# First expert's weights loaded during attention's output steps, into exchanged places of SBUF

## The chip, the cores and the metric

The kernel runs on all 8 cores of one Trainium2 chip. Each core takes one of the 8 sequences (2048 tokens of 1024 numbers) and works alone; the cores exchange nothing. The time is device microseconds of the slowest core, so a change counts only as far as it shortens the core that ends last.

## The reference

One layer: an attention block and a mixture-of-experts block, each with a layer norm before it, one after it, and a residual.

```python
x = x + layernorm(attn(layernorm(x), w_lhs, w_rhs))
x = x + layernorm(ffn(layernorm(x), ...))

def attn(x, w_lhs, w_rhs):            # one head, no projections
    scores = einsum('nsd,ntd->nst', x * w_lhs, x * w_rhs)
    return einsum('nst,ntd->nsd', softmax(scores, axis=2), x)

def ffn(xf):
    shared = silu(xf @ w1.T) * (xf @ w2.T) @ w3.T       # hidden 4096
    s = sigmoid(xf @ router_w.T)                        # 8 experts
    gates = s * one_hot(top_k(s + bias, 2)).sum(-2)     # 2 per token
    routed = sum_e((silu(h1_e) * h2_e * gate_e) @ w3_e.T)   # hidden 1024
    return shared + routed
```

## The kernel before, in words

A core's tokens are 16 tiles of 128. The program has these stages:

1. **Norm and scores** (0 to about 185 us): layer norm, transposes, attention's scores and their exponentials. The exponentials lie in four blocks `P_T[0..3]`, one for each 4 tiles; the normed tokens in `n1_tm[0..15]`.
2. **Attention's output steps** (185 to about 310 us), one for each tile `g`. `av(g)` is 48 matmuls of `P_T[g // 4]` with all of `n1_tm`. `y1` and `y2` on VectorE form the second residual stream `x2t` and its moments, with two small powers on GpSimd between them (`rsqrt`, L392); SyncE stores `x2t` to DRAM (`x2s`) and loads the input tile of step `g + 4`. `n2a` and `n2t` norm and transpose it for the FFN. From `g = 6` on, 4 tiles at a time are routed, and from `g = 8` on GpSimd writes the normed rows to their experts' places in DRAM with two indirect DMAs a tile (`scatter(g - 8)`, L694). `n2a(g)` writes a row buffer of 10, and waits until the scatter of tile `g - 10` has landed.
3. **Units and experts** (310 to about 1440 us). The shared FFN is cut into 10 units `u` of 3 or 5 hidden tiles (11 pieces of weights, `load_s_piece`). After each of the units 0 to 7 stands one expert. `p1` makes a hidden tile for 512 tokens (matmuls into `h1`, `h2`; Silu on ScalarE `sg`; the product on VectorE `SG`), `p2` multiplies by `w3` into a bank `ob`, and VectorE copies or adds the bank to the accumulator `acc[0..15]` (L828, L830). An expert runs one turn ahead of a loop and then as many turns as its rows have further blocks of 128.
4. **End**: gathers of the experts' results into `acc`, the last norm, the output.

**Where the order comes from.** Every engine's instructions are written in program order, with waits on semaphores. GpSimd has one DMA queue (queue 0, also called software dynamic): the weights are f32 in DRAM and are cast to bf16 by the DMA, and the scatters go through the same queue, behind one another. SyncE has its own (queue 1, hardware dynamic). In unit 0 the routing of the last tiles is still under way: the list `hooks` puts a piece of it behind each `p1`, among them the scatters 8 to 15, then `zeros` (8 indirect DMAs that clear the rest of each expert's last block), then `blocks_begin`: SyncE waits until every scatter and `zeros` have landed, reads 17 numbers, and loads the first expert's first block `xst` (L1077). PE needs that block at `e_X` (transposes `xps<-xst`, L889), one `p1` before the end of unit 0.

**The first expert's weights.** An expert's weights are two halves `e_all[0]`, `e_all[1]` of 12 KB a partition, 24 KB in bf16, each loaded by three DMAs of 1 MB (counted in bf16). Before the change `e_all[0]` lies at 68 to 92 KB of a partition, over `n1_tm`, which PE reads until `av(15)` has ended. So its load for expert 0 stands behind step 15 on GpSimd, ahead of the scatters 8 to 15. The second half lies at 92 to 116 KB and is loaded by `s1_load`, behind `zeros`, with the next shared piece after it. The accumulators lie at 116 to 180 KB, over `P_T[1..3]` and free input buffers.

Of the kernel before, what the change touches and what calls it, by code (L numbers as in the profile page):

```python
# [5 lines left out]
F32 = mybir.dt.float32  # L6
# [7 lines left out]
P = 128  # L14
D = 1024
# [5 lines left out]
KB = 1024  # L21
NT = 16
# [28 lines left out]
def build_program():  # L51
# [11 lines left out]
    we_d = nc.dram_tensor("we", [2 * NEXP, P, 12 * KB], F32, kind="ExternalInput").ap()  # L63
# [11 lines left out]
    def sb_at(name, shape, dtype, off):  # L75
        fb = int(np.prod(shape[1:])) * mybir.dt.size(dtype)
        assert 0 <= off and off + fb <= ARENA_B, (name, off)
        return nc.alloc_sbuf_tensor_at(name, shape, dtype, offset=SB_BASE + off)
# [19 lines left out]
    NB2 = len(n2tm)  # L98


    s_off = [32 * KB, 50 * KB, 104 * KB]
    e_off = [68 * KB, 92 * KB]

    s_all = {(sl, n): sb_at(f"sall_{sl}_{n}", [P, n * 3, KB], BF16, s_off[sl])
             for unit in UNITS for p, sl in unit for n in [S_PIECES[p]]}
# [2 lines left out]
    e_all = [sb_at(f"eall_{h}", [P, 12, KB], BF16, e_off[h]) for h in range(2)]  # L108
    e_w12 = [e_all[h][:, 0:8, :].rearrange("p (k c2) (c1 q) -> p k (c2 c1) q", k=2, q=512) for h in range(2)]
    e_w3 = [e_all[h][:, 8:12, :] for h in range(2)]  # L110
    acc = [sb_at(f"acc{i}", [P, D], F32, (116 + 4 * i) * KB) for i in range(NT)]
    ffn_off = [180 * KB]

    def sb_ffn(name, shape, dtype):
# [20 lines left out]


    NX2 = 5
    x2r = [sb_at(f"x2r{b}", [P, D], F32, (68 + 4 * b) * KB) for b in range(NX2)]
    osb = [sb_at(f"osb{b}", [P, D], F32, (88 + 4 * b) * KB) for b in range(4)]

    pp = SG_off
    def sb_seq(name, shape, dtype):
# [94 lines left out]
    def mksem(name):  # L237
        g = nc.semaphore(name)
        h = g.__enter__()
        sem_guards.append(g)  # L240
        return h
# [11 lines left out]
    S = {n: mksem(n) for n in names}  # L253
# [3 lines left out]
    def inc(s, n=1):  # L257
        cnt[_sem_name[id(s)]] += n
        return cnt[_sem_name[id(s)]]

    def cur(s):
        return cnt[_sem_name[id(s)]]
# [9 lines left out]
    def dma(eng, out_ap, in_ap, s):  # L272
        v = inc(s, 16)
        E(eng, lambda e, o=out_ap, i=in_ap, ss=s: e.dma_start(out=o, in_=i).then_inc(ss, 16))  # L274
        return v
# [11 lines left out]
    def load_table(idx):  # L287
        E("scalar", lambda e, idx=idx: e.add_instruction(
            mybir.InstLoadActFuncSet(name=nc.get_next_instruction_name(),
                                     act_func_set_id=idx, ins=[], outs=[])))  # L290
# [5 lines left out]
    def wt(eng, tok):  # L296


        if tok is None:
            return  # L300
        if tok[0] == "dec":
            E(eng, lambda e: e.wait_ge(S[tok[1]], tok[2]).then_inc(S[tok[1]], -tok[2]))  # L302
        elif tok[0] == "peek":
            W(eng, S[tok[1]], tok[2])
        elif waited.get((eng, tok[0]), 0) < tok[1]:
            waited[(eng, tok[0])] = tok[1]
            W(eng, S[tok[0]], tok[1])
# [22 lines left out]
    def load_s_piece(p):  # L330
# [4 lines left out]
            ws_d[p][:, n * 2 * KB:n * 3 * KB].rearrange("p (a b) -> p a b", b=KB), S[f"ws{sl}"])  # L335
        s_loaded[p] = (f"ws{sl}", cur(S[f"ws{sl}"]))

    def load_e_half(k, h):
        for q in range(3):
            dma("gpsimd", e_all[h][:, 4 * q:4 * q + 4, :],  # L340
                we_d[2 * k + h, :, 4 * q * KB:(4 * q + 4) * KB].rearrange("p (a b) -> p a b", b=KB),
                S[f"we{h}"])
        e_loaded[(k, h)] = (f"we{h}", cur(S[f"we{h}"]))

    s_loaded, e_loaded = {}, {}
    slot_of = {p: sl for unit in UNITS for p, sl in unit}
# [151 lines left out]
    for s in range(NT + 3):  # L498
# [10 lines left out]
        i = s - 3  # L509
# [18 lines left out]
    for g in ready:  # L528
# [6 lines left out]
    av_tok, den_tok, y_free, ry_tok, r2_tok, x2_tok, n2a_tok, tp2_tok, n2_tok, logit_tok = (  # L535
        {}, {}, {}, {}, {}, {}, {}, {}, {}, {})
# [150 lines left out]
    def scatter(i):  # L687
        b = i % NB2
        wt("gpsimd", idx_tok[i // NR])
        wt("gpsimd", n2a_tok[i])  # L690
        wt("gpsimd", z_done)
        for k in range(2):
            v = inc(S[f"sct{b}"], 16)
            E("gpsimd", lambda e, k=k: e.indirect_dma_start(  # L694
                out=xs_d[:, :], out_offset=bass.IndirectOffsetOnAxis(ap=idx[k][:, i:i + 1], axis=0),
                in_=n2tm[b][:].bitcast(I32), in_offset=None).then_inc(S[f"sct{b}"], 16))
        sct[i] = buf_free[b] = (f"sct{b}", v)
# [9 lines left out]
    for g in range(NT):  # L707
        av(g)
        y1(g)
        if g >= 1:  # L710
            n2a(g - 1)
        if g >= 6 and (g - 6) % NR == 0:
            for i in range(g - 6, g - 6 + NR):
                logits(i)
        if g >= 2:
            n2t(g - 2)
        y2(g)
        q, s = divmod(g - 6, NR)
        if q >= 0 and s == 0:
            route_a(q)  # L720
        if q >= 0 and s == 1:
            ranks(q)
        if q >= 0 and s == 2:
            route_b(q)
        if g >= 8:
            scatter(g - 8)
    load_table(TBL_SILU)

    def n2_turn(g):
# [4 lines left out]
        if g == NT - 1:  # L734
            for i in range(NT - NR, NT):
                logits(i)

    wt("gpsimd", av_tok[NT - 1])
    load_e_half(0, 0)


    BT, BX = 2, 3
# [58 lines left out]
    def p2(u, tb, b, ready):  # L801

        tiles = tiles_of[u]
        wt("tensor", ready)
        for tt in range(4):
            ti = tb * 4 + tt
            for h in range(2):
                k = banks[bank_i[0] % len(banks)]
                bank_i[0] += 1
                wt("tensor", bank_free[k])  # L810
                for j, (piece, sl, jl) in enumerate(tiles):
                    w = s_w3[sl, S_PIECES[piece]]
                    f = mm(ob[k][:], SG[b][j][:, tt * P:(tt + 1) * P], w[:, jl, h * 512:(h + 1) * 512],
                           j == 0, j == len(tiles) - 1)
                    if j == len(tiles) - 1:
                        t = put("tensor", f, "pe")
                    else:
                        E("tensor", f)
                wt("vector", t)
                a = acc[ti][:, h * 512:(h + 1) * 512]  # L820
                if u == 0 and ti == NT - 1:
                    wt("vector", x2_tok[NT - 2])
                if u == NEXP:
                    wt("vector", ya_tok[ti])
                if u == NEXP + 1:
                    wt("vector", yk_tok[ti])
                if u == 0:
                    bank_free[k] = put("vector", lambda e, a=a, k=k: e.tensor_copy(a, ob[k][:]), "dve")  # L828
                else:
                    bank_free[k] = put("vector", lambda e, a=a, k=k: e.tensor_add(a, a, ob[k][:]), "dve")  # L830
                add_tok[(u, ti)] = bank_free[k]
            if u == NSU - 1 and tb < 3:
                hooks.append(lambda ti=ti: final_stats(ti))
            elif u == NSU - 1:
                final_stats(ti)
        SG_free[b] = t
        return t
# [270 lines left out]
        state["zeros"] = ("s_zr", v)  # L1108

    def s1_load():  # L1110
        load_e_half(0, 1)
        for b in buf_free:
            wt("gpsimd", buf_free[b])
        load_s_piece(1)
# [90 lines left out]
    for u in range(NSU):  # L1205
        nt = len(tiles_of[u])
        for tb in range(4):
            b = nblk[0] % 2
            for j in range(nt):
                k = u - 1 if j == 0 and tb == 0 and 1 <= u <= NEXP else None  # L1210
# [12 lines left out]
                elif state.get("next_e") is not None:  # L1223
                    k = state.pop("next_e")
# [134 lines left out]
```

## Time and profile before

| What | Value |
|---|---|
| Time, median of 3 runs | 1485.11 us (1481.72 to 1492.14) |
| The profiled execution's own time | 1484.35 us |
| Its slowest core (core 5), span | 1482.8 us |
| The other cores' spans | 1455.5 to 1474.4 us |
| PE busy on core 5 | 1386.6 us, 94% |
| PE's granted clock, mean of core 5 | 0.983 |

The profile's page is of core 5. PE, the matrix engine, is the busy one. What one stage costs is read from its own stretch of the timeline; "idle before" in brackets is the time an engine stood still ahead of a row, and the name behind it what released it. The row of slices cuts the span in 40 slices of 37 us.

### The profile page before, as it was taken

To read this page: it belongs to the slowest core of one execution; us is meant where nothing else is said; L and a number is where in the kernel's file an instruction comes from. 1 tells how busy PE (TensorE), PEld (TensorE's weight loads), DVE (VectorE), ACT (ScalarE), POOL (GpSimd) and SP (SyncE) were. 2 spreads that over 40 slices of the span, in tenths; PEclk is the share of its full clock that TensorE was granted. 3 is DMA by queue.
4 is the path that set the end of the run, shared out by engine and by line. 5 is a ranking of instruction groups with operands and counts; after the bars stand their busy time and mean duration, and the time that the engine had idled before them with its cause. 6 is when DMAs were issued, how large, how long until landed. Compare 5 with 4: busy or idle time off the path is not lost. (4 is left out here: it accounts for less than half of the span.)

```text
span 1482.8 us, 21476 instructions; the slowest of 8 cores (1455.5 to 1482.8 us)
## 1 busy us (share of the span) xinstructions
PE 1386.6 (94%) x7324; PEld 644.1 (43%) x7324; DVE 606.0 (41%) x1208; ACT 288.5 (19%) x423; POOL 235.7 (16%) x245
## 2 busy tenths in 40 slices
PE   3999999996999999999999999999999997999993
PEld 2443345542444444444444444444444443444431
DVE  5520067864422223532243444344235341243557
ACT  4642311120012211012111111111211101211123
POOL 5510011354000001000101010000010222033236
PEclk9999999998999999999999999999999998999997
DMA  7910073559712216611484749191186899486235
GB/s 203 284 44 1 0 178 125 180 138 253 129 50 77 72 64 155 116 50 64 119 172 93 164 78 178 46 199 40 68 166 105 164 204 217 126 165 114 86 114 185
DMA packets 46224, 184.82 MB, mean 125 GB/s; under 512 B 6208, under 2 KB 6208, under 8 KB 38592
## 3 DMA queue, kind: packets, MB, share of 16 engines
q0 software_dynamic: 18464, 103.05, 35.9%
q1 hardware_dynamic: 27680, 80.72, 16.2%
q8 instruction: 49, 0.80, 0.2%
q14 instruction: 31, 0.25, 0.1%
HBM read 203.61 MB, written 55.75 MB: 175 GB/s over the span
## 5 line engine op out<-in xcount | busy, mean ns | idle before, releaser
L323 PE MATMUL ob<-sall,SG 128*128 128x512 bf16 x1024 | 235.0, 386 | 16.0 <-DVE acc L830 7.2
L830 DVE TENSOR_TENSOR acc<-acc,ob 128x512 f32<-128x512 f32 x288 | 187.0, 686 | 9.6 <-PE ob L323 8.2
L323 PEld LDWEIGHTS ob<-sall,SG 128*128 128x128 bf16 x1024 | 101.1, 99 | 143.1 <-issue 27.7
L274 POOL DMA_DIRECT2D eall<-we x48 | 25.7, 557 | 770.6 <-PE h1pb L323 769.5
L323 PE MATMUL ob<-eall,GT 128*128 128x512 bf16 x592 | 136.0, 384 | 0.0
L323 PE MATMUL h1pb<-n2fm,sall 128*128 128x512 bf16 x512 | 122.8, 383 | 9.3 <-DVE SG L790 9.3
L790 DVE TENSOR_TENSOR SG<-sg,h2pb 128x512 bf16<-128x512 f32 x64 | 44.0, 687 | 211.4 <-PE h2pb L323 183.4
L323 PE MATMUL stp<-n1fm,afm 128*128 128x512 bf16 x512 | 123.3, 384 | 0.0
L323 PE MATMUL h1pa<-n2fm,sall 128*128 128x512 bf16 x512 | 122.4, 382 | 0.6 <-DVE SG L790 0.6
L323 PE MATMUL h2pb<-n2fm,sall 128*128 128x512 bf16 x512 | 121.4, 380 | 0.0
L323 PE MATMUL h2pa<-n2fm,sall 128*128 128x512 bf16 x512 | 121.2, 380 | 0.0
L323 PE MATMUL avp<-n1tm,pt 128*128 128x512 bf16 x512 | 118.8, 377 | 0.0
L790 DVE TENSOR_TENSOR SG<-sg,h2pa 128x512 bf16<-128x512 f32 x64 | 44.0, 688 | 152.6 <-PE h2pa L323 144.1
L781 ACT ACTIVATE sg<-h1pb 128x512 f32<-128x512 f32 x64 | 38.1, 595 | 273.0 <-PE h1pb L323 257.3
L323 PEld LDWEIGHTS ob<-eall,GT 128*128 128x128 bf16 x592 | 57.4, 99 | 64.6 <-issue 2.9
L929 DVE COPY GT<-tps 128x1024 bf16<-128x1024 bf16 x37 | 25.6, 692 | 142.7 <-DVEq L302 142.7
L781 ACT ACTIVATE sg<-h1pa 128x512 f32<-128x512 f32 x64 | 38.1, 596 | 226.6 <-PE h1pa L323 211.6
L323 PEld LDWEIGHTS h1pb<-n2fm,sall 128*128 128x128 bf16 x512 | 50.3, 99 | 70.9 <-issue 12.2
L323 PE MATMUL h1pa<-eall,xT 128*128 128x512 bf16 x296 | 69.9, 379 | 11.5 <-PEq L302 11.5
L323 PEld LDWEIGHTS h2pb<-n2fm,sall 128*128 128x128 bf16 x512 | 50.3, 98 | 61.0 <-issue 1.1
L323 PEld LDWEIGHTS h1pa<-n2fm,sall 128*128 128x128 bf16 x512 | 49.9, 98 | 60.6 <-issue 2.4
L323 PEld LDWEIGHTS h2pa<-n2fm,sall 128*128 128x128 bf16 x512 | 49.9, 98 | 59.0 <-issue 0.8
(129 smaller groups left out, 1402.1 us busy)
## 6 DMA issues: line engine op xcount, KB each, us to landing
eall<-we POOLq DMA_DIRECT2D x48, 1024.0 KB, 27.2
ys<-ysb SPq DMA_DIRECT2D x37, 512.0 KB, 2.7
xr<-x SPq DMA_DIRECT2D x32, 512.0 KB, 8.1
sall<-ws POOLq DMA_DIRECT2D x10, 1536.0 KB, 39.1
xst<-xs SPq DMA_DIRECT2D x39, 260.0 KB, 2.8
ys<-zrow SPq DMA_DIRECT2D x16, 512.0 KB, 9.1
x2s<-x2t SPq DMA_DIRECT2D x16, 512.0 KB
x2r<-x2s SPq DMA_DIRECT2D x16, 512.0 KB, 4.2
```

Of the source, the lines that this page charges most:

```text
L274: E(eng, lambda e, o=out_ap, i=in_ap, ss=s: e.dma_start(out=o, in_=i).then_inc(ss, 16))
L323: return lambda e: e.matmul(out, lhsT, rhs, start=start, stop=stop, skip_group_check=True)
L781: ta = put("scalar", lambda e: e.activation(sg[pr][:], hp[pr][0][:], ACT.Silu), "act")
L790: tv = put("vector", lambda e: e.tensor_mul(SG[b][j][:], sg[pr][:], hp[pr][1][:]), "dve")
L830: bank_free[k] = put("vector", lambda e, a=a, k=k: e.tensor_add(a, a, ob[k][:]), "dve")
L929: give("vector", lambda e: e.tensor_copy(GT[:], tps[:]), "cr_gt")
```

## The change

- The accumulators `acc[0..7]` move to 68 to 100 KB, the place of `n1_tm`; `acc[8..15]` stay. The expert's halves move to 100 to 124 KB (over `P_T[0]` and half of `P_T[1]`) and 124 to 148 KB (the rest of `P_T[1]`, and `P_T[2]`). The third place for shared pieces and the buffers of the last stage (`x2r`, `osb`) move with them.
- The first half of expert 0 is loaded in three single DMAs of 1 MB behind the scatters of the steps 9, 10 and 11, once `av(7)` has ended; the second half likewise in the steps 13, 14 and 15, once `av(11)` has ended.
- The old loads behind step 15 and in `s1_load` are gone. VectorE's first copy into `acc` names a wait for `av(15)`; VectorE has waited for it already in step 15, and no instruction is added.

```diff
-    s_off = [32 * KB, 50 * KB, 104 * KB]
-    e_off = [68 * KB, 92 * KB]
+    s_off = [32 * KB, 50 * KB, 136 * KB]
+    e_off = [100 * KB, 124 * KB]
...
-    acc = [sb_at(f"acc{i}", [P, D], F32, (116 + 4 * i) * KB) for i in range(NT)]
+    acc = [sb_at(f"acc{i}", [P, D], F32, ((68 if i < 8 else 116) + 4 * i) * KB) for i in range(NT)]
...
-    x2r = [sb_at(f"x2r{b}", [P, D], F32, (68 + 4 * b) * KB) for b in range(NX2)]
-    osb = [sb_at(f"osb{b}", [P, D], F32, (88 + 4 * b) * KB) for b in range(4)]
+    x2r = [sb_at(f"x2r{b}", [P, D], F32, (100 + 4 * b) * KB) for b in range(NX2)]
+    osb = [sb_at(f"osb{b}", [P, D], F32, (120 + 4 * b) * KB) for b in range(4)]
...
+    def load_e_part(k, h, q):
+        dma("gpsimd", e_all[h][:, 4 * q:4 * q + 4, :],
+            we_d[2 * k + h, :, 4 * q * KB:(4 * q + 4) * KB].rearrange("p (a b) -> p a b", b=KB),
+            S[f"we{h}"])
+        e_loaded[(k, h)] = (f"we{h}", cur(S[f"we{h}"]))
+
     def load_e_half(k, h):
         for q in range(3):
...
+            load_e_part(k, h, q)
...
         if g >= 8:
             scatter(g - 8)
+
+        if 9 <= g <= 11:
+            wt("gpsimd", av_tok[7])
+            load_e_part(0, 0, g - 9)
+        if g >= 13:
+            wt("gpsimd", av_tok[11])
+            load_e_part(0, 1, g - 13)
...
-    wt("gpsimd", av_tok[NT - 1])
-    load_e_half(0, 0)
...
+                if u == 0 and ti == 0:
+                    wt("vector", av_tok[NT - 1])
...
     def s1_load():
-        load_e_half(0, 1)
         for b in buf_free:
```

**GpSimd in the steps 9 to 11.** `ry` and `r` are the two small powers of a step, `xs<-n2tm` its scatters, `eall<-we` a weight DMA. Before:

```order
L392 TENSOR_TENSOR ry<-vey,mhalf 128x1 [waits dve]
L392 TENSOR_TENSOR r_204<-ve_203,mhalf 128x1 [waits dve]
L694 DMA xs<-n2tm_83,idx_189 17664x520 [waits act]
L694 DMA xs<-n2tm_83,idx_190 17664x520
L392 TENSOR_TENSOR ry<-vey,mhalf 128x1 [waits dve]
L392 TENSOR_TENSOR r_204<-ve_203,mhalf 128x1 [waits dve]
```

After:

```order
L395 TENSOR_TENSOR ry<-vey,mhalf 128x1 [waits dve]
L395 TENSOR_TENSOR r_204<-ve_203,mhalf 128x1 [waits dve]
L697 DMA xs<-n2tm_83,idx_189 17664x520 [waits act]
L697 DMA xs<-n2tm_83,idx_190 17664x520
L274 DMA eall_103<-we 128x4096 [waits pe]
L395 TENSOR_TENSOR ry<-vey,mhalf 128x1 [waits dve]
```

One weight DMA stands between a step's scatters and the next step's `ry`; it is so in six steps.

**GpSimd in unit 0, behind the scatters 12 to 15.** Before:

```order
L694 DMA xs<-n2tm_87,idx_190 17664x520
L1105 DMA xs<-zrows,idz 17664x520 [waits dve]
L1105 DMA xs<-zrows,idz 17664x520 x7
L274 DMA eall_104<-we 128x4096 x3
L274 DMA sall_3_101<-ws 128x6144 [waits sct0,sct1,sct2,sct3,sct4,sct5,sct6,sct7,sct8,sct9]
L274 DMA sall_3_101<-ws 128x3072
```

After:

```order
L697 DMA xs<-n2tm_87,idx_190 17664x520
L1114 DMA xs<-zrows,idz 17664x520 [waits dve]
L1114 DMA xs<-zrows,idz 17664x520 x7
L274 DMA sall_3_101<-ws 128x6144 [waits sct0,sct1,sct2,sct3,sct4,sct5,sct6,sct7,sct8,sct9]
L274 DMA sall_3_101<-ws 128x3072
```

The three weight DMAs between `zeros` and the next shared piece are gone, as are the three that stood ahead of scatter 8. The instructions of PE, VectorE, ScalarE and SyncE, and their waits, stand in the same order as before.

## Rows read from the trace of the kernel before

**Rows 1.** The page, core 5: span, and DMA in 40 slices.
```profile
span 1482.8 us, 21476 instructions; the slowest of 8 cores (1455.5 to 1482.8 us)
...
DMA  7910073559712216611484749191186899486235
```
**Rows 2.** Cores: span and mean granted clock.
```profile
core 0: 1473.9 us, clock 0.975
...
core 5: 1482.8 us, clock 0.983
```
**Rows 3.** Timeline, PE, core 5, unit 0: start, duration, instructions [idle before <-releaser].
```profile
310.87 1.89 PE L323 MATMUL h1pa<-n2fm,sall 128*128 128x512 bf16 x8
...
351.59 1.89 PE L323 MATMUL h2pa<-n2fm,sall 128*128 128x512 bf16 x8
362.79 3.57 PE L323 MATMUL h1pb<-n2fm,sall 128*128 128x512 bf16 x8 [9.31 <-DVE SG L790]
366.16 2.33 PE L323 MATMUL h2pb<-n2fm,sall 128*128 128x512 bf16 x8
...
396.39 1.89 PE L323 MATMUL h1pa<-eall,xT 128*128 128x512 bf16 x8 [2.07 <-PEq L302]
```
**Rows 4.** Timeline, VectorE, core 5, where PE stands still.
```profile
361.96 0.69 DVE L790 TENSOR_TENSOR SG<-sg,h2pb 128x512 bf16<-128x512 f32 x1 [14.70 <-remote]
```
**Rows 5.** Timeline, PE, core 0, `e_X` and what follows it.
```profile
384.94 1.01 PE L889 MATMUL xps<-idnb,xst 128*128 128x128 bf16 x8 [7.66 <-PEq L302]
...
393.20 1.89 PE L323 MATMUL h1pa<-eall,xT 128*128 128x512 bf16 x7 [2.06 <-PEq L302]
```
**Rows 6.** Timeline, PE, core 4, the same place.
```profile
386.46 0.61 PE L889 MATMUL xps<-idnb,xst 128*128 128x128 bf16 x8 [1.05 <-PEq L302]
...
392.59 1.89 PE L323 MATMUL h1pa<-eall,xT 128*128 128x512 bf16 x8 [2.06 <-PEq L302]
```
**Rows 7.** Core 0: SyncE's wait for `zeros`, its first `xst` load, issue to landing.
```profile
SPq L270 <- DMA xs<-zrows,idz: 9.9, 1, 9.9
...
L1077 SPq DMA_DIRECT2D xst<-xs x1: 332/332/332, 371.1 to 371.1; - x1
...
xst<-xs SPq DMA_DIRECT2D x1, 260.0 KB, 13.7
```
**Rows 8.** Timeline, GpSimd, core 5, from the end of attention.
```profile
303.15 0.97 POOL L694 DMA_INDIRECT xs<-n2tm,idx  x1 [0.27 <-issue]
304.15 0.57 POOL L392 TENSOR_TENSOR ry<-vey,mhalf 128x1 f32<-128x1 f32 x1
...
320.78 1.71 POOL L274 DMA_DIRECT2D eall<-we  x3
...
356.92 0.96 POOL L1105 DMA_INDIRECT xs<-zrows,idz  x1 [0.27 <-issue]
357.87 1.70 POOL L274 DMA_DIRECT2D eall<-we  x3
359.51 1.11 POOL L274 DMA_DIRECT2D sall<-ws  x2
```
**Rows 9.** Busy time by stretch, core 5; at the end clock, DMA share, GB/s.
```profile
246.00:310.00 64.00, 63.47 (x515) 32.94 (x514) 51.52 (x165) 10.09 (x10) 21.96 (x29) 1.00 0.45 158
...
330.00:343.00 13.00, 8.35 (x44) 3.49 (x43) 7.80 (x35) 0.72 (x2) 5.64 (x6) 1.00 1.00 160
343.00:358.00 15.00, 10.48 (x41) 4.22 (x39) 3.36 (x6) 0.60 (x1) 11.76 (x14) 0.85 1.02 354
358.00:400.00 42.00, 34.09 (x153) 15.00 (x154) 18.48 (x36) 4.18 (x7) 2.63 (x5) 0.89 0.98 172
```
**Rows 10.** Timeline, core 5, steps 11 to 15: the store of tile 11, `y2(13)`, `av(15)`.
```profile
283.26 0.33 SPq L274 DMA_DIRECT2D x2s<-x2t  x1
...
297.70 1.28 DVE L573 SCALAR_TENSOR_TENSOR x2t<-avp,ry,xr 128x1024 f32<-128x1024 f32 x1 [1.02 <-POOL ry L392]
...
302.31 0.59 PE L323 MATMUL avp<-n1tm,pt 128*128 128x512 bf16 x2
```

More of the change, by code:

```diff
@@ L336, in load_s_piece @@
         s_loaded[p] = (f"ws{sl}", cur(S[f"ws{sl}"]))
+    def load_e_part(k, h, q):
[3 more added lines that the diff above has]
+        e_loaded[(k, h)] = (f"we{h}", cur(S[f"we{h}"]))
     def load_e_half(k, h):
         for q in range(3):
[L340 to L343, printed above, removed]
+            load_e_part(k, h, q)
     s_loaded, e_loaded = {}, {}
```

## Prediction

> **What bounds the kernel now.** I read the page first, then the cores, then PE's timeline where attention ends and unit 0 runs, and last the DMA queues there. The page gives 1482.8 us for the slowest core [rows 1]; it is core 5, 9 us behind core 0 [rows 2]. Nothing passes between the cores, so the gain has to be found on core 5, and the next ones must not stay behind above it. The slices of DMA show two loads of work: 7 to 4 tenths while attention's output steps run (slices 5 to 8, 185 to 333 us), then 9 and 7 while unit 0 runs [rows 1]. By stretch it is plainer: share 0.45 in the steps, 1.00 from 330 to 343 us, 1.02 to 358 us and 0.98 to 400 us [rows 9]. So the queues are full exactly where the routing has to get its rows out, and half empty just before.
>
> PE has no wait on weights of the first expert. What the full queues cost it shows in two forms, and a core has one or the other.
>
> Form A, core 5: PE stands still for 9.31 us, released by VectorE's product `SG` at 362.79 us, and VectorE itself stood for 14.70 us ahead of that product, released by "remote", an update that no instruction of the core is named for [rows 3, 4]. This lies at the end of the stretch in which the scatters and `zeros`, held up behind the first half's weights, drain at 354 GB/s [rows 9]. Behind the pause PE's next two groups take 3.57 and 2.33 us, where two undisturbed ones take 1.89 each [rows 3]; the granted clock of 343 to 358 us is 0.85 against 1.00 ahead of it [rows 9]. Full speed is the 2.4 GHz level, so part of the stretch ran at 1.2.
>
> Form B, core 0: no pause there, but PE waits 7.66 us at `e_X` for the first block `xst`, against 1.05 us on core 4 [rows 5, 6]. SyncE waits 9.9 us for the last of `zeros`, issues the load at 371.1 us, and it lands 13.7 us later, beside the weights of the second half and of piece 1 [rows 7]. A core with form A comes to `e_X` late enough not to see B.
>
> **What the change removes.** Six DMAs of 1 MB leave this stretch: three issued at 320.78 us ahead of scatter 8, three at 357.87 us behind `zeros` [rows 8]. At 160 GB/s, the rate of a stretch with weights alone [rows 9], 1.05 MB take 6.6 us of all engines, so 39 us of DMA leave. What is left of unit 0 is 16 scatters and 8 `zeros`, which GpSimd issues one by one; the last is issued at 356.92 us [rows 8] and now finds an empty queue, and behind it piece 1 alone (9 x 1024 numbers of 2 bytes on 128 partitions, 2.36 MB).
>
> - Form A on core 5. PE's groups were 8 matmuls; the group at 351.59 us would have been followed at about 353.4 us and was followed at 362.79 us. That is 9.4 us, and the slow groups 3.57 + 2.33 - 2 x 1.89 = 2.1 us more. Removed: **11.5 us**, if the cause is the drain of the held-up queue. Bounds: 0, if it comes from the number of scatters and not from their being held up, and 11.5.
> - Would B come up instead? `zeros` then end about 2 us behind their last issue, at 360 us on core 5. On core 0 the wait for `zeros` was 9.9 us; so much earlier the load of `xst` goes out, at about 362 us there and at 364 on core 5. Even if it takes the 13.7 us of [rows 7], it lands at 378. PE on core 5, with 11.5 us less, reaches `e_X` 8.2 us before the expert's first matmul: core 0 took 8.26 us between them and core 4 took 6.13 [rows 5, 6], so at about 396.4 - 11.5 - 6.1 = 378.8 us. B costs 0 to 1 us; since only piece 1 is beside it I take 0.
> - Core 0: 7.66 - 1.05 = 6.6 us of waiting and 8.26 - 6.13 = 2.1 us of slow matmuls behind it go, 8.7 us. From 1473.9 it comes to 1465; core 5 stays the slowest. Unit 0 on core 5 took from 310.87 to 396.39 us, 85.5 us, and comes to 74.0.
>
> **What the change adds.** Six DMAs in attention's steps, on GpSimd and on the engines.
>
> - GpSimd: 1.70 us for three [rows 8], 0.57 us for one. In step 14 `ry` starts at 304.15 us, at once when the scatter is over [rows 8], so it is late by 0.57 us, and `y2` with it. PE needs `y2(13)`, over at 297.70 + 1.28 = 298.98 us, when `av(15)` starts at 302.31 us [rows 10]: 3.3 us of room. Cost 0. The Trainium skill, SBUF — State Buffer, section SBUF: two separate sides, has a rule against such a place: while VectorE runs an instruction in a two-port mode, GpSimd can't write its DMAs' descriptors; the section on the bandwidth-pool intuition gives 0.62 us for such a DMA alone and 3.1 us beside a VectorE copy. VectorE is busy 51.52 of 64 us there, yet a scatter takes 0.97 us in it and 0.96 us in the quiet stretch [rows 8, 9]; the trace speaks against the rule here. By it six issues would be 2.5 us longer, within the 3.3 us.
> - The engines: a step of 7.8 us (125 us by 16) has 0.45 x 7.8 = 3.5 us of DMA [rows 9]. With 6.6 us it has 10.1. Six such steps are 14 us over; step 12 without a load gives back 4.3. So some 10 us of queue 0 are left when attention ends, and are gone by about 334 us, before the scatters 12 to 15. A scatter on whose landing `n2a` waits is issued two steps before, 15.6 us, against at most 10 us of queue. Cost 0.
> - SyncE's stores of `x2t`. The store of tile 11 is issued at 283.26 us, and `y2(13)` overwrites its buffer at 297.70 us [rows 10]: 14.4 us of room, and 3.3 more until PE feels it. Nothing shows such a store beside weights; the nearest row is `xst`, also one piece for each of 128 partitions, 13.7 us [rows 7]. The step's load of `x` stands ahead in the same queue and could double that: 27.4 - 14.4 - 3.3 = 9.7 us late at the worst, in one or two of the steps (loads of `x` end with step 11). Below nothing there is no bound to name: a busier queue makes no step shorter. I take 0.5 us, nearer to the `xst` row, because the queues are empty for a third of a step before the first weight DMA.
> - Exchanged places and VectorE's named wait: no instruction more. Cost 0; piece 10 and the last stage's buffers wait for the same event as before.
>
> **Sum.** 1484.35 - 11.5 + 0.5 = 1473.4 us against the profiled execution's own time. The median of the runs is 0.8 us above it, so the forecast is **1474 us**, 0.75% below the median.
>
> **The rivals.**
>
> - *R1, form A stays.* The updates of cores with form A come late because 24 indirect DMAs land close together, not because they were held up. For it: the stretch at 354 GB/s is theirs [rows 9]; against it: issued one by one, each of 0.27 MB in 0.96 + 0.27 us [rows 8], they move at 216 GB/s and no longer at 354. Then core 5 stays at 1484 to 1485 us, or if half of it goes, at 1479. Chance 0.17.
> - *R2, late stores.* Two steps lose 5 us each (half of the worst above) and 2.1 us of slow matmuls behind the pause: 1474 + 10 to 14 = 1484 to 1488. For it: `xst`'s 13.7 us of the 14.4; against it: the scatters' packets are short. Chance 0.12.
> - *R3, DMA sets the pace of the steps, and the kernel is slower.* If SyncE's stores wait for everything in queue 0, each of the six steps takes 10.1 us in place of 7.8, 13.8 us in all, and PE pauses in each and falls to its lower level, as behind the pause in [rows 3]; with 2.1 us behind each, 26 us. 1474 + 26 = 1500 us, or 1488 with the pauses alone. It decides from 11 us on. Against it: `xst`, 128 packets, landed beside a full queue 0, so the queues take turns. The Trainium skill, DMA: Bandwidth & Descriptors, section Queues, rings and completion order, says that an engine changes queues only after a whole packet, typically 9 to 17 descriptors. By that a store could be passed over by a whole weight DMA, 6.6 us, at each turn, which speaks for this rival. Chance 0.10.
> - *R4, more than the sum.* The profiled execution shows one case of form A. Core 0 shows form B, and the runs of before reach 1492 us. If form A costs the slowest core more in the timed runs than in the profiled one, or hits a second time later, the gain is 16 to 20 us: 1466 to 1469. Against it: nothing in the trace says so. Chance 0.10.
> - That the change doesn't do what it says is excluded by the order of the instructions.
>
> **The numbers.** About 1% is what a measurement of this kernel can tell from no change; 1% is 14.9 us, so faster means below 1470.3. My forecast (chance 0.51) lies 4 us above that line with a spread of some 4 us, so a quarter to a third of it falls below: 0.16. With R4 that is 0.26 for faster. R3 gives slower 0.05, the pauses alone fall within 1%. The rest, 0.69, is within 1%. The range that holds 8 in 10 goes from 1466 (R4's edge) to 1487 (R1 and most of R2).
>
> **What would show it.** Right: on core 5 the first expert matmul some 74 us after the first of unit 0 and no PE pause above 5 us between; `xps<-xst` with 1.05 us idle on all cores; SyncE's load of `xst` near 362 us; DMA share near 1 from 272 to 334 us; the steps as long as before. A pause by "remote" near 355 us would show R1; idle ahead of `x2t<-avp` that ends with a DMA, R2; matmuls `avp` at the lower clock in the steps 12 to 15, R3. Wrong altogether would be a wait of PE for `eall` in expert 0.

## The result and the profile after

The changed kernel takes 1491.58 us (median of 20 runs, 1482.22 to 1734.32), the kernel before 1484.34 us (20 runs beside it). The ratio is 1.0052, 95% interval 1.0029 to 1.0074: slower by half a per cent, inside the 1% that counts as no change, and outside the forecast range of 1466 to 1487. In some executions the cores of one die run at a lower granted clock and the time is several per cent longer; every ratio leaves these out, the medians of all runs do not. The profiled execution took 1491.67 us; its slowest core is core 5 again, 7.3 us behind the value of [rows 2], while core 0 got 4.2 us faster. The spans of cores 0 and 5:

```profile
core 0: 1469.7 us, clock 0.977
...
core 5: 1490.1 us, clock 0.982
```

The timeline of PE on core 5, where [rows 3] stood (start, duration, instructions, idle before and releaser; the first row is the count of the last four tiles' experts, ahead of unit 0):

```profile
316.90 0.19 PE L323 MATMUL logit<-M,ltri 128*128 128x32 bf16 x1 [5.69 <-DVE M L654]
...
358.72 1.89 PE L323 MATMUL h2pa<-n2fm,sall 128*128 128x512 bf16 x8
368.86 3.57 PE L323 MATMUL h1pb<-n2fm,sall 128*128 128x512 bf16 x8 [8.25 <-DVE SG L797]
372.22 2.91 PE L323 MATMUL h2pb<-n2fm,sall 128*128 128x512 bf16 x8
```

Ahead of the first of these rows PE stood 0.52 us before the change:

```profile
310.74 0.18 PE L323 MATMUL logit<-M,ltri 128*128 128x32 bf16 x1 [0.52 <-DVE M L651]
```

Expert 0 starts at 403.04 us, 6.6 us later than in [rows 3]. Unit 0 starts 6.2 us later (317.03 against 310.87), takes 86.0 us in place of 85.5, and the rest of the program 1087.1 in place of 1086.4. So the pause that was to go is there: 8.25 us for 9.31, with two slow groups behind it again (3.57 and 2.91 us for 3.57 and 2.33). VectorE shows the same wait as in [rows 4], and ScalarE has one too:

```profile
368.02 0.69 DVE L797 TENSOR_TENSOR SG<-sg,h2pb 128x512 bf16<-128x512 f32 x1 [13.75 <-remote]
```
```profile
367.19 0.60 ACT L788 ACTIVATE sg<-h1pb 128x512 f32<-128x512 f32 x1 [26.00 <-remote]
```

Yet the queue is no longer full there. The stretches of core 5, columns as in [rows 9]:

```profile
246.00:300.00 54.00, 52.86 (x414) 27.04 (x411) 42.32 (x136) 8.76 (x8) 19.21 (x26) 1.00 0.75 186
300.00:311.00 11.00, 11.00 (x111) 6.10 (x109) 4.98 (x15) 1.32 (x2) 3.73 (x5) 1.00 1.00 222
311.00:330.00 19.00, 11.64 (x95) 5.88 (x93) 15.12 (x56) 4.84 (x5) 8.46 (x11) 0.91 1.02 202
330.00:343.00 13.00, 11.35 (x57) 4.94 (x56) 5.02 (x31) 4.45 (x6) 6.14 (x7) 1.00 1.01 269
343.00:358.00 15.00, 10.90 (x39) 4.20 (x37) 8.15 (x24) 0.00 (x0) 10.55 (x11) 0.77 0.54 210
358.00:400.00 42.00, 32.70 (x146) 14.15 (x144) 16.92 (x33) 4.18 (x7) 5.95 (x7) 0.88 0.46 101
```

The load moved as the change says: share 1.00 to 1.02 from 300 to 343 us, 0.54 and 0.46 behind it, where before it was 1.02 and 0.98. The late start of unit 0 has its cause in VectorE's timeline, step 14 on core 5:

```profile
299.33 1.28 DVE L576 SCALAR_TENSOR_TENSOR x2t<-avp,ry,xr 128x1024 f32<-128x1024 f32 x1 [1.05 <-POOL ry L395]
...
311.00 1.28 DVE L576 SCALAR_TENSOR_TENSOR x2t<-avp,ry,xr 128x1024 f32<-128x1024 f32 x1 [5.56 <-DMA x2s<-x2t]
```

The first row is `y2(13)`, the second `y2(14)`. It waits 5.56 us for the store of tile 12, which SyncE issued at 292.01 us, so that store took 19 us to land. The stores of `x2t` from issue to landing on core 0 (DMA view, stretch 270 to 316 us, last column the median), before and after:

```profile
x2s<-x2t SPq DMA_DIRECT2D x6, 512.0 KB, 2.8
```
```profile
x2s<-x2t SPq DMA_DIRECT2D x5, 512.0 KB, 14.0
```

On core 0, form B went as forecast: the wait for `xst` is 1.06 us, as it was on core 4 in [rows 6], and expert 0 starts at 386.66 us, 6.5 us earlier than in [rows 5] although unit 0 began 1.8 us later. (2.3 us of that went again in the rest of the program; its mean granted clock, 0.977 for 0.975, doesn't explain that.) The load of `xst` went out at 366.96 us, not near 362 as forecast: the last of `zeros` was issued 3.9 us later than before (its issue ends at 359.6 us for 355.7), and the load took 10.9 us to land in place of 13.7.

```profile
380.54 0.61 PE L898 MATMUL xps<-idnb,xst 128*128 128x128 bf16 x8 [1.06 <-PEq L302]
...
386.66 1.67 PE L323 MATMUL h1pa<-eall,xT 128*128 128x512 bf16 x6 [2.06 <-PEq L302]
```

### The profile page after: what moved, and what is told of

The parts are those of the page before. It is cut to its first block and busy times, and to the rows that moved or that the text cites. A ratio compares the mean times of both kernels' runs of the same rounds, so it can differ in the third digit from the quotient of the medians.

```text
span 1490.1 us, 21477 instructions; the slowest of 8 cores (1450.9 to 1490.1 us)
## 1 busy us (share of the span) xinstructions
PE 1387.8 (93%) x7324; PEld 644.3 (43%) x7324; DVE 606.0 (41%) x1208; ACT 288.4 (19%) x423; POOL 236.1 (16%) x245
## 5 line engine op out<-in xcount | busy, mean ns | idle before, releaser
L797 DVE TENSOR_TENSOR SG<-sg,h2pb 128x512 bf16<-128x512 f32 x64 | 44.0, 688 | 210.9 <-PE h2pb L323 184.0
L323 PE MATMUL h1pa<-eall,xT 128*128 128x512 bf16 x296 | 69.9, 379 | 11.5 <-PEq L302 11.5
## 6 DMA issues: line engine op xcount, KB each, us to landing
ys<-zrow SPq DMA_DIRECT2D x16, 512.0 KB, 11.5
```

Of the source, the lines that this page charges most:

```text
L323: return lambda e: e.matmul(out, lhsT, rhs, start=start, stop=stop, skip_group_check=True)
L797: tv = put("vector", lambda e: e.tensor_mul(SG[b][j][:], sg[pr][:], hp[pr][1][:]), "dve")
```

## The experiments

In unit 0 GpSimd issues indirect DMAs 1.23 us apart in two rows without a gap: the *first chain* (scatters 8 to 11, 8 DMAs) and the *second chain* (scatters 12 to 15 and `zeros`, 16 DMAs). What follows the start of expert 0 takes core 5 between 1083 and 1088 us in all 18 traces, so that start is the measure. Four chips were used: A for e1 to e4, B for e5 to e8, C for e9 to e12, D for e13 to e16. Every ratio is to the kernel before on the same chip. Pause: PE's longest single idle time between the start of the second chain and `e_X`, without the 2.8 to 4.3 us for `acc` or `idz` that every core has once as that chain begins; wait: that of `xps<-xst`; both are the range over the four cores of a die in the profiled execution ("1" is the usual 1.05, "0" is under 0.4).

| Run | Median us | Ratio to before, 95% | 2nd chain | Pause, cores 0-3 / 4-7 | Wait, cores 0-3 / 4-7 |
|---|---|---|---|---|---|
| before, first trace | 1484.3 | 1 | 16 | 0 / 3.2 to 9.7 | 5.9 to 7.7 / 1 |
| changed, first trace | 1491.6 | 1.0052 (1.0029, 1.0074) | 16 | 0 / 6.4 to 10.1 | 1 / 1 |
| e1 places only | 1485.1 | 1.0013 (0.9989, 1.0037) | 16 | 0 / 11.7 to 13.6 | 6.4 to 8.4 / 1 |
| e2 first half early | 1492.7 | 1.0075 (1.0053, 1.0096) | 16 | 0 / 3.9 to 10.0 | 1 to 1.8 / 1 |
| e3 second half early | 1484.9 | 1.0011 (1.0001, 1.0022) | 16 | 0 / 4.9 to 12.4 | 11.9 to 13.7 / 1 to 6.6 |
| e4 six loads spread | 1489.2 | 1.0045 (1.0029, 1.0062) | 16 | 0 / 2.5 to 9.4 | 1 / 1 |
| e5 before, no zeros | 1473.8 | 0.9918 (0.9895, 0.9941) | 8 | 0 / 0 | 1 to 4.2 / 1 to 2.7 |
| e6 changed, no zeros | 1478.0 | 0.9952 (0.9933, 0.9971) | 8 | 0 / 0 | 1 / 1 |
| e7 spread, no zeros | 1474.1 | 0.9915 (0.9889, 0.9940) | 8 | 0 / 0 | 1 / 1 |
| e8 spread, chain broken | 1484.4 | 0.9987 (0.9961, 1.0013) | 8+4+4 | 0 / 0 to 13.1 | 3.6 to 4.8 / 1 to 3.2 |
| e9 before, SyncE's zeros | 1488.2 | 1.0026 (1.0006, 1.0046) | 8 | 0 / 0 | 15.9 to 21.9 / 9.9 to 16.6 |
| e10 spread, SyncE's zeros | 1473.3 | 0.9943 (0.9917, 0.9969) | 8 | 0 / 0 | 1 to 2.3 / 1 |
| e11 e10 in pairs | 1484.5 | 0.9990 (0.9966, 1.0014) | 4 x 2 | 0 / 0 | 4.8 to 11.5 / 9.0 to 11.3 |
| e12 before, more zeros | 1486.7 | 1.0028 (1.0012, 1.0043) | 24 | 3.3 to 19.5 / 0 | 1 / 11.3 to 12.5 |
| e13 before | 1481.1 | 0.9997 (0.9974, 1.0020) | 16 | 4.0 to 9.4 / 0 | 1 / 5.9 to 7.1 |
| e14 changed | 1488.0 | 1.0051 (1.0034, 1.0068) | 16 | 7.1 to 10.4 / 0 | 1 / 1 |
| e15 changed, more zeros | 1498.8 | 1.0124 (1.0081, 1.0168) | 24 | 7.3 to 24.0 / 0 | 1 / 8.5 to 8.9 |
| e16 changed, SyncE's zeros | 1474.8 | 0.9966 (0.9945, 0.9987) | 8 | 0 / 0 | 1 to 2.5 / 1 |

### Which part of the change (e1 to e4)

**e1, the places alone**, both loads at their old points:

```diff
+    wt("gpsimd", av_tok[NT - 1])
+    load_e_half(0, 0)
...
     def s1_load():
+        load_e_half(0, 1)
```

> The exchanged places alone: accumulators and expert halves as in the change, but both halves loaded where they were before. Theory S (late stores): the weight DMAs in the output steps make the whole loss there, so this kernel equals the one before, 1484 us, first matmul of unit 0 at 311 us on core 5, unit 0 85 us. Rival P (places): other addresses slow PE, VectorE or the DMAs; then part of the 0.5% loss stays, 1488 to 1491 us.

Measured 1.0013, within 0.4% at the most: no cost of the places shows. The traced execution was one of the longer ones (1492.4 us), with pauses of 11.7 to 13.6 us at the same 16 DMAs. One trace gives a pause only to some 4 us.

**e2, the first half early alone**, the second back in `s1_load`:

```diff
-        if g >= 13:
-            wt("gpsimd", av_tok[11])
-            load_e_part(0, 1, g - 13)
...
     def s1_load():
+        load_e_half(0, 1)
```

> Only the first half is loaded in the output steps 9 to 11; the second half behind the zeros as before. Theory S: the store of tile 12, issued behind the load of x of step 11 and beside the weights of step 11, is already late here: y2(14) waits 3 to 5 us for it on some cores, unit 0 begins 3 to 6 us late on cores 4 to 7. Rival S2 (the weights of step 13 do it): no wait for a store, unit 0 begins at 311 to 312 us. Unit 0: the first half's weights no longer stand ahead of scatters 8 to 15. Theory I (the indirect DMAs themselves hold up the updates of cores 4 to 7): the pause of 8 to 10 us stays on them; rival H (only the held-up queue does it): it goes and core 5 ends at 1474 to 1478 us. The first block xst is loaded beside four weight DMAs again, so cores 0 to 3 wait 0 to 3 us at e_X.

Over the timed runs core 5 has a median of 1491.1 us against 1481.5 before, core 0 1459.8 against 1467.0. Core 7 went from 1473.1 to 1480.8 us. On seven cores `y2(14)` waits 2.0 to 3.9 us for a store. This half alone brings the whole loss of cores 5 and 7, and the gain of cores 0 to 3.

**e3, the second half early alone**, the first behind step 15:

```diff
-        if 9 <= g <= 11:
-            wt("gpsimd", av_tok[7])
-            load_e_part(0, 0, g - 9)
...
+    wt("gpsimd", av_tok[NT - 1])
+    load_e_half(0, 0)
```

> Only the second half is loaded in the output steps 13 to 15; the first half behind step 15 as before. Theory S: no store is late (queue 0 is empty until step 13, and no load of x stands ahead of the stores any more); unit 0 begins at 311 to 312 us. Rival S2: y2(14) or y2(15) still waits 3 us or more for a store. Unit 0: scatters 8 to 15 are held up as before or more, so the pause on cores 4 to 7 stays (theories I and H alike), and cores 0 to 3 wait for xst less than the 6 to 7.7 us of before, 0 to 4 us. Total 1482 to 1487 us.

Measured 1.0011, and no `y2` waits for a store; cores 0 to 3 now wait 11.9 to 13.7 us for `xst`, longer than before. So it is the first half, ahead of the scatters, that makes form B, and not the second half beside `xst`.

**e4, the six loads spread** over the steps 5, 7, 9, 11, 13, 15:

```diff
-        if 9 <= g <= 11:
...
-        if g >= 13:
...
+        if g >= 5 and g % 2 == 1:
+            k = (g - 5) // 2
+            wt("gpsimd", av_tok[(3, 3, 7, 7, 11, 11)[k]])
+            load_e_part(0, k // 3, k % 3)
```

> The six weight DMAs one in each second step: steps 5, 7, 9, 11, 13 and 15, the first two as soon as av(3) has ended. Two steps then hold 7 us of DMA of their own and 6.6 us of weights in 15.6 us. Theory S: no step waits for a store, unit 0 begins at 311 to 313 us on all cores, so 4 to 6 us of the change's loss on cores 5 to 7 go. Theory I: the pause in unit 0 stays on cores 4 to 7, so core 5 stays at 1482 to 1486 us, cores 0 to 3 are 7 to 9 us shorter than before. Rival H: the pause goes with the held-up queue, core 5 at 1473.

No wait of `y2` for a store is left, unit 0 starts on core 5 at 311.8 us, and core 5 takes 1487.5 us (median) all the same. Late stores are a part of the loss; the pause on core 5 is still 9.27 us.

### What makes the pause (e5 to e8)

**e5, e6, e7: zeros out of the chain**, in the kernel before, in the changed one, and in e4. SyncE clears the 57 blocks in stage 1 with plain DMAs. The list `cleared` holds the blocks that this input leaves part-filled on some core, so these three are no versions for other inputs.

```diff
+            cleared = [e * XS_STRIDE + k for e, ks in {...}.items() for k in ks]
-            for z in range(NEXP * XS_STRIDE, XS_BLOCKS):
+            for z in cleared + list(range(NEXP * XS_STRIDE, XS_BLOCKS)):
...
-        wt("sync", state["zeros"])
...
-              then(... (scatter, (15,)), (zeros, ()), (blocks_begin, ()), ...),
+              then(... (scatter, (15,)), (blocks_begin, ()), ...),
```

> The kernel before, but the 8 indirect DMAs of zeros are gone: SyncE clears the blocks that may end part-filled (57 of them, listed from this input's counts) with plain DMAs during stage 1, 15 MB more there. GpSimd's chain of back-to-back indirect DMAs in unit 0 is 8 long in place of 16. Theory T1 (on cores 4 to 7 the other engines' semaphore updates come late while GpSimd issues a long chain of indirect DMAs, whatever the queue holds): the chain ends near 348 us in place of 358, the pause of core 5 before h1pb or h2pb shrinks from 9.3 us to under 3, cores 4 to 7 start expert 0 8 to 11 us earlier, slowest core near 1473, ratio 0.993 to 0.995. Theory T2 (the pause is the drain of scatters held up behind 3 MB of weights): the weights are still ahead of the scatters, so the pause stays above 6 us and cores 4 to 7 gain under 3 us. Under both, core 0 gains its wait for xst, about 7 us.

The weights still stood ahead of the scatters, and the pause is gone on all eight cores, though the queue is as full as in [rows 9] (share 1.04 from 343 to 358 us on core 5). Core 5 in the profiled execution:

```profile
378.14 0.61 PE L890 MATMUL xps<-idnb,xst 128*128 128x128 bf16 x8 [1.05 <-PEq L302]
384.27 1.89 PE L323 MATMUL h1pa<-eall,xT 128*128 128x512 bf16 x8 [2.06 <-PEq L302]
```

Expert 0 starts 12.1 us earlier than in [rows 3], and the median of core 5 went from 1482.2 to 1469.3 us, 12.9 us. This is the 11.5 us of form A, and it comes from taking away indirect DMAs, not weights. T2 fell.

> The changed kernel with zeros taken away in the same way. T1: the pause behind the chain (8.3 us on core 5, 10.1 on core 7) falls under 3 us, slowest core 1487.6 - 8 = about 1480. T2 (pause from held-up scatters) is already in trouble, since the queue is not full in the changed kernel; by it nothing changes, 1488. Attention's late stores stay, about 5 us on core 5. A third possibility, T3: the 15 MB cleared in stage 1 lengthen that stage; then attention's output steps begin later than 183 us on all cores.

Right for the time. T3 is out: `av(0)` starts at 182.5 to 184.0 us, against 181.9 to 183.5 in the first trace of the kernel before. Core 7 shows a wait of 7.00 us at `logit<-M` behind the *first* chain, and starts expert 0 at 398.4 us.

> The six 1 MB loads in the steps 5, 7, 9, 11, 13, 15, and zeros taken away as in the two others. T1: core 5 from 1487.5 (loads spread, zeros in place) to about 1478, cores 0 to 3 unchanged near 1458, so the time is near 1479, ratio 0.996. If R2's late stores are the larger cost and T1 false: no change against 1489.

1474.1 us, 5 us better than expected, 4 us under e6 and level with e5: without `zeros` the moved weights gain nothing on the slowest core. Core 6 waits 5.84 us behind the first chain.

**e8, the chain broken** in the spread kernel:

```diff
         wt("gpsimd", state["tab"])
+        wt("gpsimd", sct[NT - 1])
         for k in range(NEXP):
+            if k == 4:
+                wt("gpsimd", ("s_zr", v))
```

> The six loads spread, zeros in place, but GpSimd waits until scatter 15 has landed before zeros, and until the first four of zeros have landed before the other four: the chain of 16 indirect DMAs becomes 8, 4 and 4 with some 2 us between. T1: updates get through in the breaks, no PE pause above 5 us on cores 4 to 7, in place of one of 9; the last zeros are issued 4 to 5 us later, which no one waits for on these cores. Core 5 gains 3 to 7 us against the same without breaks: 1481 to 1485. T4 (the total of indirect DMAs in this stretch counts, not their standing back to back): the pause comes in two pieces with the same sum, or stays, 1487 to 1490.

Mixed. Cores 4 and 5 have no pause and core 5's median is 6.6 us under that of e4 (1480.9 for 1487.5, on another chip), but core 7 has one of 13.05 us, longer than without breaks. Two breaks of 2.6 us do not cure it reliably, and `xst` comes 2 to 4 us too late on the other cores.

### Zeros on another queue (e9 to e11), and more of them (e12)

**e9, SyncE writes the zeros**; it reads the eight rows into registers:

```diff
     def blocks_begin():
+        wt("sync", state["tab"])
+        ends = [nc.alloc_register(nc.sync.engine, f"end{k}") for k in range(NEXP)]
+        def clear(k):
+            def f(e):
+                e.reg_load(ends[k], idz[0:1, k:k + 1])
+                r = bass.RuntimeValue.of_register_unchecked(ends[k], min_val=0, max_val=(XS_BLOCKS - 1) * P)
+                e.dma_start(out=xs_d[bass.ds(r, P), :], in_=zrows[:]).then_inc(S["s_zr"], 16)
+            return f
+        for k in range(NEXP):
+            zv = inc(S["s_zr"], 16)
+            E("sync", clear(k))
...
-        wt("sync", state["zeros"])
+        wt("sync", ("s_zr", zv))
...
-              then(... (scatter, (15,)), (zeros, ()), (blocks_begin, ()), ...),
+              then(... (scatter, (15,)), (blocks_begin, ()), ...),
```

> The kernel before, but the 8 blocks of zeros are written by SyncE with plain DMAs, whose rows it reads from idz once VectorE has made it; nothing is added in stage 1 and no list from this input is used. GpSimd's second chain is 8 indirect DMAs long in place of 16. T1 (the length of the chain, and not the bytes cleared, holds up the updates on cores 4 to 7): no pause above 5 us behind the chain, core 5 near 1470 to 1474, all of the gain that taking zeros away gave on cores 4 to 7; ratio 0.992 to 0.995. T5 (the bytes that zeros write beside the scatters and weights cause the pause): the pause stays, core 5 at 1480 to 1483.

The pause is gone on all cores, as T1 said, but the time was missed: every core now waits for `xst`, 9.9 to 21.9 us. Core 5:

```profile
393.14 1.01 PE L889 MATMUL xps<-idnb,xst 128*128 128x128 bf16 x8 [13.68 <-PEq L302]
```

Form B took the place of form A. The expectation had left out that the scatters are still held up behind the first half: the next shared piece, which waits for them, is issued at 367.74 us.

**e10**, e9's edit on the spread loads.

> The same with the six 1 MB loads in the steps 5, 7, 9, 11, 13, 15. T1: like the variant with the blocks cleared in stage 1, 1472 to 1476; the moved loads gain 7 to 10 us on cores 0 to 3 and nothing on the slowest core, since on some of cores 4 to 7 the first chain (scatters 8 to 11, 8 indirect DMAs behind one another, now without weights ahead of them) delays the ranks of the last tiles by 5 to 10 us.

1473.3 us, valid for any input, 0.6% below the kernel before on the same chip, which is still inside the 1% taken as no change. Core 5 in the profiled execution has neither pause nor wait and starts expert 0 at 387.2 us. From e9 to e10 the moved weights take the ratio from 1.0026 to 0.9943, 12 us. The first chain cost a wait of 4.96 us on core 1, not on cores 4 to 7 as forecast. And the die is not free of the delay: behind its own plain DMAs SyncE waits 11.3 to 17.1 us for the last to land on cores 0 to 3, and 1.3 to 1.5 us on cores 4 to 7, and issues the load of `xst` at 370.6 to 382.7 us there against 357.8 to 360.2. Cores 0 and 4:

```profile
SPq L270 <- DMA xs<-zrows: 11.3, 1, 11.3
```
```profile
SPq L270 <- DMA xs<-zrows: 1.3, 1, 1.3
```

PE waits 2.3 us for `xst` at the most, so this costs little here.

**e11, pairs**: on top of e10

```diff
         wt("gpsimd", z_done)
+        if i > 8:
+            wt("gpsimd", sct[i - 1])
```

> Zeros by SyncE, loads spread, and each scatter of tiles 9 to 15 waits until the scatter before it has landed: no chain longer than two indirect DMAs anywhere, with some 2.6 us between pairs, as in attention's steps, where no late update is seen. T1: no wait for a late update above 2 us on any core in unit 0, cores 5, 6 and 7 start expert 0 at 384 to 387 us, slowest core 1467 to 1470, ratio 0.990. If the number of indirect DMAs in the stretch decides and not their standing back to back, one of cores 5 to 7 still shows a wait of 10 to 15 us and the time is as without pairs. The scatters end some 20 us later, near 361 us, and xst is loaded a few us behind them; a wait of up to 3 us at xps is possible on all cores.

PE has no wait for a late update; its one idle time without a named cause is 0.76 us, so the first half held. The price was set too low: the last scatter's issue ends at 366.5 to 370.8 us, not 361, and the wait for `xst` is 4.8 to 11.5 us.

**e12, 8 more indirect DMAs** behind `zeros` in the kernel before:

```diff
+    xz_d = nc.dram_tensor("xz", [XS_BLOCKS * P, DG // 2], I32, kind="Internal").ap()
...
-        for k in range(NEXP):
+        for k in range(2 * NEXP):
...
-                out=xs_d[:, :], ...ap=idz[:, k:k + 1]...
+                out=(xs_d if k < NEXP else xz_d)[:, :], ...ap=idz[:, k % NEXP:k % NEXP + 1]...
```

> The kernel before with 8 further indirect DMAs of zrows behind zeros, into a tensor that nobody reads: the second chain is 24 long in place of 16. T1: on cores 4 to 7 the pause grows by about the 8 x 1.23 = 9.8 us, to 19 us before h1pb on core 5; cores 0 to 3 show no such pause, and only a later xst (about 5 to 10 us). Slowest core 1490 to 1493. T2 (held-up weights and scatters): the pause stays 9 us, the time is 1484 to 1487.

Wrong about the cores: this chip shows the pause on cores 0 to 3 and none on 4 to 7. Both rows follow: core 1's pause, and core 5, which waits for `xst` instead. The pause did grow with the chain, but the time by less than forecast, since the die with the slowest core was the other one:

```profile
370.38 3.41 PE L324 MATMUL h1pb<-n2fm,sall 128*128 128x512 bf16 x8 [16.56 <-DVE SG L791]
```
```profile
388.17 1.01 PE L890 MATMUL xps<-idnb,xst 128*128 128x128 bf16 x8 [12.51 <-PEq L303]
```

### The count of indirect DMAs, on one chip (e13 to e16)

**e13 and e14** are the kernel before and the changed kernel, unedited; **e15** is the changed kernel with e12's edit, **e16** with e9's.

> The kernel before once more, for a trace from the same chip as the next three. If late updates hit a fixed set of cores, cores 4 to 7 show the pause behind the second chain again, 9 to 14 us, and cores 0 to 3 none. If the set changes with the chip or the execution, another group shows it. Time 1482 to 1485.

> The changed kernel once more on the same chip: 1488 to 1492, the pause behind the second chain (scatters 12 to 15 and zeros) on the same cores as in the kernel before, and idle time of 3 to 6 us ahead of y2(14), ended by the landing of a store of x2t, on most cores.

> The changed kernel with 8 further indirect DMAs of zrows into a tensor that nobody reads: the chain is 24 long, and no weights are in the queue. If the length of the chain sets the pause: 9.8 us longer than in the changed kernel on the cores that show it, 18 to 20 us, slowest core near 1498. If the held-up queue set it, the pause stays 8 to 10 us.

> The changed kernel as it is, loads in the steps 9 to 11 and 13 to 15, with zeros written by SyncE. The chain is 8 long: the pause behind the second chain is gone, core 5 gains 8 to 14 us on the changed kernel. What is left against the spread loads with zeros by SyncE (1473.2) is the price of six loads in seven steps, the late stores of x2t: 4 to 6 us by the trace of the changed kernel, so 1476 to 1479.

The pause of core 1 in e13 (16 DMAs), e14 (16, weights moved) and e15 (24, weights moved), one fence each:

```profile
363.38 3.57 PE L323 MATMUL h1pb<-n2fm,sall 128*128 128x512 bf16 x8 [9.39 <-DVE SG L790]
```
```profile
377.84 3.57 PE L323 MATMUL h1pb<-n2fm,sall 128*128 128x512 bf16 x8 [10.42 <-DVE SG L797]
```
```profile
385.20 3.39 PE L324 MATMUL h1pb<-n2fm,sall 128*128 128x512 bf16 x8 [21.00 <-DVE SG L798]
```

Eight DMAs more, 9.8 us of issue, add 10.6 us of pause on core 1; on cores 2 and 3 they add 14.7 us each (7.14 to 21.84 and 9.33 to 23.98), and on core 0 the pause breaks into five, 7.28 us the longest. The ratio goes from 1.0051 to 1.0124, 10.8 us. In e16, with 8, core 1 has none. That the same cores show it on each chip was wrong: here it is cores 0 to 3 in e13, e14 and e15 alike. Core 5, on the die without the pause, had waited for `xst` in e13 and does not in e14:

```profile
383.45 1.01 PE L889 MATMUL xps<-idnb,xst 128*128 128x128 bf16 x8 [6.03 <-PEq L302]
```
```profile
385.47 1.89 PE L323 MATMUL h1pa<-eall,xT 128*128 128x512 bf16 x8 [2.06 <-PEq L302]
```

So on chip D core 5 gained 5.6 us (median 1477.8 to 1472.2) and core 1 lost 12.0 (1472.9 to 1484.9) and became the slowest. Core 1's loss begins ahead of the second chain:

```profile
316.63 0.18 PE L323 MATMUL logit<-M,ltri 128*128 128x32 bf16 x1 [5.99 <-DVE M L654]
342.90 0.18 PE L323 MATMUL logit<-M,ltri 128*128 128x32 bf16 x1 [7.20 <-DVE M L654]
```

The first row is the late store (VectorE idle 5.84 us ahead of `y2(14)`, ended by `x2s<-x2t`). The second is behind the first chain: VectorE had stood 11.63 us for a late update there, `idx` came late, and the second chain was issued to 372.1 us in place of 358.4. In e13 this matmul has no wait, but the chain delays core 1 there too, by less. VectorE and, a few matmuls on, PE:

```profile
335.00 0.69 DVE L790 TENSOR_TENSOR SG<-sg,h2pb 128x512 bf16<-128x512 f32 x1 [3.33 <-remote]
```
```profile
337.10 1.46 PE L323 MATMUL ob<-sall,SG 128*128 128x512 bf16 x6 [0.78 <-DVE base L680]
```

## Why the prediction was wrong

- **"Removed: 11.5 us, if the cause is the drain of the held-up queue."** This is the step that failed. It took the full queue of [rows 9] for the cause because both stood in the same 15 us. The bound of 0 beside it, "if it comes from the number of scatters and not from their being held up", is what the runs bear out (R1, given 0.17). Shown: the pause is there with a half-empty queue (e14, share 0.22 and 0.56 from 343 to 370 us on core 1), is gone with a full one and half the chain (e5, e9), and grows by 10.6 us with 9.8 us more of chain (e15, core 1). Its size was right: e5 got 12.9 us on core 5. The rivals were priced one at a time; the result is R1 and a part of R2 together, and lies above the 1484 to 1485 us of R1 and the 1484 to 1488 of R2.
- **"SyncE's stores: I take 0.5 us."** Mis-sized, inside its own bounds of 0 and 9.7. The path was wrong too: the 3.3 us of room was read at `y2(13)` and `av(15)`, but the store that came late held up `y2(14)`, behind which VectorE makes `M` for the count of the last four tiles, and PE's wait for `M` grew from 0.52 to 5.69 us on core 5. A store of `x2t` took 14.0 us where it had taken 2.8; the `xst` row of 13.7 us had said so, and I let "the queues are empty for a third of a step" talk it down. Step 14 cost 5.56 us on core 5 and up to 6.1 elsewhere. Over the whole kernel the tight placing costs less than that, or less than the 4 to 6 us I expected of e16: 1474.8 us against 1473.3 for e10, on another chip. The Trainium skill, DMA: Bandwidth & Descriptors, section Queues, rings and completion order, has an engine change queues only after a whole packet; a store beside weight DMAs that takes 14.0 us in place of 2.8 agrees with it, though nothing here shows packet by packet that this is the reason.
- **"Cost 0" for the scatters and for GpSimd's issues.** Two costs were missing. `ry` comes some 0.6 us later behind a load, and VectorE's wait for it grows by that at `y2(10)` (1.55 for 0.94 us, core 5) and at `y2(12)` (0.98 for 0.36). PE does feel it: cores 0 and 4, without a store wait, start unit 0 1.8 and 2.7 us late. The Trainium skill's rule on descriptors beside a two-port mode (SBUF — State Buffer, section SBUF: two separate sides) did not show: a weight DMA's issue takes 0.60 us in the steps. No run here shows whether a VectorE instruction in such a mode stood beside one. And the weights ahead of the first chain had a use that the prediction did not list: with them gone, one or two cores of the affected die wait 2.9 to 7.2 us at `logit<-M` behind that chain as well (the changed kernel, e2, e4, e6, e7, e8, e10, e14, e15). With the weights there (before, e1, e3, e5, e9, e12, e13) this matmul waits under 0.6 us. They do not keep the chain's delay away: in these runs most cores of the affected die wait 0.5 to 4.0 us for `base` there. And e16, without the weights, shows no such wait at `logit<-M` and 1.8 us at most for `base`. Late store, first chain and second chain are core 1's loss in e14; why the first chain costs less with the weights ahead is open.
- **Core 0, "8.7 us go".** Right for unit 0, which took 82.5 us and takes 74.1, 8.4 us less; the span came to 1469.7 us, not 1465, by the late start of 1.8 us and the 2.3 us in the rest. It was worth nothing for the time, since the other die was the slowest.
- **"A core with form A comes to `e_X` late enough not to see B."** Right for all cores with a pause above 0.4 us in the 18 traces but for cores 4 and 5 of e3 (pauses of 4.90 and 4.95 us, waits of 6.38 and 6.60), and it explains the result. On one die updates are late and PE pauses (A); on the other PE waits for `xst` (B). The change takes away B alone, and puts its costs on both.
- R3 did not happen: `avp` ran at full clock, 1.00 from 246 to 311 us. R4 did not either.

A third buffer for `x2t` was not tried, so the share of the stores is read from the traces and from e4. Whether the number of DMAs standing back to back decides, or their number in the whole stretch, is not settled either: 8 + 4 + 4 with breaks of 2.6 us still gave 13.05 us on one core (e8), and the runs without a pause have fewer indirect DMAs as well. Open are what in a chain delays the updates, and what chooses the die: cores 4 to 7 in the first traces and on chips A and B, cores 0 to 3 on C and D.

## What to carry to other kernels

Two things that stand in the same stretch (a full queue, a pause) are not yet cause and effect: when a page shows "remote" behind a row of indirect DMAs, count the DMAs, and try fewer of them before moving other traffic. Price a move by the cores that set the time, and check on each die which form of a loss they have: here moving the weights was worth 12 us (e9 to e10) when every core waited for `xst`, nothing (e5 to e7) when no core waited over 4.2 us for it, and cost 7 us while the die with the slowest core had the pause. Spread loads over steps rather than packing them beside stores with two buffers, and look for what the moved work had been sheltering.

## What the runs showed of the hardware

- While GpSimd issues indirect DMAs 1.23 us apart, the other engines' waits on one die end late. At 8 in the second chain and none behind it PE has no pause above 0.4 us; at 16 the pause is 9.4 to 13.6 us on the worst core of each trace, at 24 it is 19.5 to 24.0. The first chain, also of 8, does delay: up to 7.2 us on PE and 11.63 on VectorE (e14). The long pauses end 2 to 10 us behind the issue of the last DMA (5 us on core 5 before and after the change). Which die shows it changed between chips.
- The same blocks written by SyncE as plain DMAs, 8 of 0.27 MB, left PE without a pause (e9, e10, e16), and took SyncE 7.7 to 13.0 us to issue. SyncE itself then waited 11.3 to 17.1 us for the last of them on one die and 1.3 to 1.5 on the other (e10; in e16 14.3 to 16.1 us on cores 1 to 3, 1.5 to 1.7 on the others).
- A 0.5 MB store in another queue than the weights went from 2.8 to 14.0 us beside 1 MB weight DMAs, which took 15.6 us themselves (medians of core 0); where the loads stood one in two steps it was 10.1 us (e10, core 5).
